# Mixing stage of a two-layer block on Trainium2: chunk states linked by a fading factor, and a turn that waits for less

## What is computed

```
q = layernorm(x);  k = v = ctx
log_D[s,t] = cums[s+1] - cums[t+1] + igate[t]   for t <= s, else -inf   (cums: running sum of log_sigmoid(fgate))
D  = exp(log_D - max_t log_D)
C  = (q k^T / 8) * D
h  = (C / (max(|sum_t C|, exp(-max log_D)) + 1e-6)) v
x += normalised h * outnorm_weight
```

## Time and profile before

| | us |
|---|---|
| median of 3 runs | 1862.72 (1861.0 to 1865.55) |
| the profiled execution, its own time | 1861.19 |
| span of that execution in the trace | 1859.5 |
| PE busy | 1683.3 (91%) |
| DVE busy | 1192.0 (64%) |
| ACT busy | 842.8 (45%) |
| POOL busy | 619.9 (33%) |

### The profile page before, as it was taken

One profiled execution on the slowest core, in us unless ns is written; L12 is line 12 of the kernel. 1 busy time (PEld: TensorE's weight loads), 2 busy tenths in 40 slices (PEclk: granted clock), 3 DMA queues, 4 the chain that ended last, 5 costly groups with the idle time before them and its releaser, 6 DMA issues. The chain is left out here.

```text
span 1859.5 us, 26060 instructions
## 1 busy us (share of the span) xinstructions
PE 1683.3 (91%) x8890; PEld 1152.6 (62%) x8890; DVE 1192.0 (64%) x2642; ACT 842.8 (45%) x1870; POOL 619.9 (33%) x746
## 2 busy tenths in 40 slices
PE   6469999996999999999999999999999999873584
PEld 4357777764666666666666666666666666572352
DVE  6444454432777777777777777777777777667761
ACT  3324443431555555555555555555555555421110
POOL 2154444430333232333333233232323232210375
PEclk9669999997999999999999999999999999955797
DMA  7100000003323222232323223232322223144144
GB/s 258 21 22 13 12 12 1 1 0 105 69 46 69 53 61 64 51 69 46 69 48 67 56 58 68 46 69 46 68 51 64 58 57 69 23 146 132 44 85 57
DMA packets 66657, 109.46 MB, mean 59 GB/s; under 512 B 16088, under 2 KB 48096, under 8 KB 66528
## 3 DMA queue, kind: packets, MB, share of 16 engines
q1 hardware_dynamic: 60384, 99.29, 21.8%
q0 software_dynamic: 6144, 8.52, 2.8%
HBM read 27.84 MB, written 12.85 MB: 22 GB/s over the span
## 5 line engine op out<-in xcount | busy, mean ns | idle before, releaser
L1030 POOL TENSOR_SCALAR at_Pr<-at_Pr,at_rinv 128x512 f32<-128x512 f32 x512 | 354.1, 692 | 826.7 <-DVE at_rinv L1057 826.7
L1009 ACT ACTIVATE at_Pr<-at_ps,at_nmax 128x512 f32<-128x512 f32 x512 | 352.0, 687 | 522.7 <-DVE at_nmax L1052 521.1
L1052 DVE TENSOR_REDUCE at_nmax<-at_ps 128x1 f32<-128x512 f32 x512 | 350.9, 685 | 139.0 <-PE at_ps L917 128.0
L917 PE MATMUL at_ps<-at_k,at_q 128*128 128x512 f32 x1024 | 420.8, 492 | 9.7 <-DMA at_k<-at_k_own 8.0
L928 PE MATMUL at_ps<-k_ident,at_Pr 128*128 128x128 f32 x2048 | 310.5, 274 | 4.0 <-POOL at_Pr L1030 4.0
L928 PEld LDWEIGHTS at_ps<-k_ident,at_Pr 128*128 128x128 f32 x2048 | 249.5, 140 | 93.2 <-POOL at_Pr L1030 32.8
L1064 DVE COPY at_PT<-at_ps 128x512 f32<-128x512 f32 x384 | 261.3, 681 | 0.0
L917 PEld LDWEIGHTS at_ps<-at_k,at_q 128*128 128x128 f32 x1024 | 174.6, 191 | 129.6 <-issue 120.1
L938 PE MATMUL at_ps<-at_PT,at_V 128*64 128x512 f32 x1024 | 233.8, 598 | 0.9 <-DVE at_PT L1064 0.9
L1057 DVE RECIPROCAL at_rinv<-at_rsum 128x1 f32<-128x1 f32 x512 | 83.3, 163 | 174.5 <-ACT at_Pr L1009 172.5
L938 PEld LDWEIGHTS at_ps<-at_PT,at_V 128*64 128x64 f32 x1024 | 67.7, 136 | 121.5 <-issue 120.3
(11 more groups left out here) (237 smaller groups left out, 2030.5 us busy)
## 6 DMA issues: line engine op xcount, KB each, us to landing
at_k<-at_k_own SPq DMA_DIRECT2D x256, 256.0 KB, 4.1
k_x<-in_x SPq DMA_DIRECT2D x8, 512.0 KB, 7.8
mg_ctx<-in_ctx SPq DMA_DIRECT2D x8, 512.0 KB, 8.0
mx_ctxn<-in_ctx SPq DMA_DIRECT2D x8, 512.0 KB, 3.9
rows<-lo_xn SPq DMA_DIRECT2D x8, 512.0 KB, 3.0
out<-k_x SPq DMA_DIRECT2D x1, 4096.0 KB, 14.6
r_w<-in_L_ffn_w SPq DMA_DIRECT2D x16, 256.0 KB, 5.6
mx_w<-in_L_ffn_w SPq DMA_DIRECT2D x2, 1024.0 KB, 9.8
```

The lines of the kernel that those rows point to most:

```text
L917: ins = pe.matmul(ps[:, S_BANK + j % 2, :], q2[:, u % 2, h, q:q + P], k2[:, u % 2, h, part, :], start=part == 0, stop=part == 1)
L1009: act.activation(Pr[:, j % 4, :], ps[:, S_BANK + j % 2, :], ACT.Exp, bias=nmax[:, j % 4:j % 4 + 1], accum_out=rsum[:, j % 4:j % 4 + 1]).th ...
L1030: pool.tensor_scalar(Pr[:, n % 4, :], Pr[:, n % 4, :], rinv[:, n % 4:n % 4 + 1], 1.0, ALU.mult, ALU.mult).then_inc(s["pn"], 1)
L1052: dve.tensor_reduce(nmax[:, j % 4:j % 4 + 1], ps[:, S_BANK + j % 2, :], AX.X, ALU.max, negate=True).then_inc(s["nmax"], 1)
```

## The change

It makes each state from the one before it. `states` computes only what each chunk adds (3 matmuls of one key tile each, weighted for the chunk's own end), and DVE adds to each the state before it times a fading factor, with two `scalar_tensor_tensor` instructions, each behind a wait for the one before. The factor is the decay's last column of each chunk, copied by `scale_queries` out of the bank that `spread_decay` filled. For that, `spread_decay` and `scores` move ahead of `states` on PE, `scale_queries` ahead of `keep_states` on DVE (and ahead of the input side's statistics), and `mapped(b, 3, 0)` ahead of the output side's turn. That turn waits for the first of the second unit's three `state` counts, the one instruction that reads U_BANK; `values` waits for all. The weights `aa`, the transposes and `weigh_keys` shrink to one tile per chunk.

```diff
-KIND_G, KIND_FLOOR, KIND_A = 0, TPB, (2 * TPB, 2 * TPB + 1, 2 * TPB + 3)
-KINDS = 2 * TPB + 6
+KIND_G, KIND_FLOOR, KIND_A = 0, TPB, 2 * TPB
+KINDS = 3 * TPB - 1
...
-                for k in range(6):
-                    at = R * (KIND_A[0] + k)
+                for k in range(TPB - 1):
+                    at = R * (KIND_A + k)
                     pe.transpose(ps[:, COL_BANK, at:at + R], aa[:, k, :], ident[0:R, 0:R])
...
-                    act.activation(aa[:, (0, 1, 3)[t]:(1, 3, 6)[t], :].rearrange("r a p -> r (a p)"),
-                                   gg[:, 0:P * (t + 1)], ACT.Exp, bias=neg_r[:, t:t + 1])
+                    act.activation(aa[:, t, :], gg[:, P * t:P * t + P], ACT.Exp, bias=neg_r[:, t:t + 1])
...
+    LINKS = TPB - 1
+        fade = sb("fade", [P, 2, TPB - 2], F32)
...
                 def states(m, p):
                     pe.wait_ge(s["kw"], m + 1)
                     pe.wait_ge(s["va"], m + 1)
-                    wait_count(pe, s["qs"], PAIRS * m + p)
-                    for k in range(TPB - 1):
-                        for t in range(k + 1):
-                            at = KIND_A[k] - KIND_A[0] + t
-                            ins = pe.matmul(ps[:, U_BANK, PV * k:PV * k + PV], kw[:, at, P * p:P * p + P],
-                                            vaug[:, t, 2 * p:2 * p + 2, :].rearrange("p h d -> p (h d)"),
-                                            start=t == 0, stop=t == k)
+                    pe.wait_ge(s["qs"], PAIRS * m + p + 1)
+                    for t in range(TPB - 1):
+                        ins = pe.matmul(ps[:, U_BANK, PV * t:PV * t + PV], kw[:, t, P * p:P * p + P],
+                                        vaug[:, t, 2 * p:2 * p + 2, :].rearrange("p h d -> p (h d)"),
+                                        start=True, stop=True)
                     ins.then_inc(s["u_ps"], 1)
...
                 def spread_decay(m, p):
-                    pe.wait_ge(s["state"], PAIRS * m + p + 1)
+                    wait_count(pe, s["state"], LINKS * (PAIRS * m + p))
...
                 def values(m, p):
-                    pe.wait_ge(s["qs"], u + 1)
+                    pe.wait_ge(s["state"], LINKS * (u + 1))
...
                     if mix:
                         spread_max(m, 0)
-                        states(m, 0)
+                        spread_decay(m, 0)
+                        scores(m, 0)
                     if mlp:
                         mapped(b, 0, 1)
                     if mix:
                         spread_max(m, 1)
+                        states(m, 0)
                     if mlp:
                         mapped(b, 1, 0)
-                    if mix:
-                        spread_decay(m, 0)
-                        scores(m, 0)
-                    if mlp:
                         mapped(b, 1, 1)
...
                         spread_max(m, 3)
-                        states(m, 1)
+                        spread_decay(m, 1)
+                        scores(m, 1)
                     if mlp:
                         mapped(b, 2, 1)
                     if mix:
-                        spread_decay(m, 1)
-                        scores(m, 1)
+                        states(m, 1)
                     done = min(m + 1, B)
+                    if mlp:
+                        mapped(b, 3, 0)
                     wait_count(pe, s["exp"], MH * done)
-                    wait_count(pe, s["qs"], PAIRS * done)
+                    wait_count(pe, s["state"], LINKS * PAIRS * done - LINKS + 1)
                     if there(b - 1):
                         wait_count(pe, s_in["out"], min(b + 1, B))
                         wait_count(pe, s_out["out"], b - 1)
                         turn(s_out, b - 1, tmp_out)
-                    if mlp:
-                        mapped(b, 3, 0)
                     if mix:
                         values(m, 1)
...
-                    for k in range(TPB - 1):
-                        at = KIND_A[k] - KIND_A[0]
...
-                        ins = pool.tensor_tensor(
-                            kw[:, at:at + k + 1, :].rearrange("p t (h d) -> p t h d", h=MH),
-                            ctxn[:, m % 2, 0:k + 1, :].rearrange("p t (h d) -> p t h d", h=MH), w, ALU.mult)
-                    ins.then_inc(s["kw"], 1)
...
+                    pool.tensor_tensor(
+                        kw[:, :, :].rearrange("p t (h d) -> p t h d", h=MH),
+                        ctxn[:, m % 2, 0:TPB - 1, :].rearrange("p t (h d) -> p t h d", h=MH), w, ALU.mult
+                    ).then_inc(s["kw"], 1)
...
                 def keep_states(m, p):
                         [P, TPB - 1, PV]), ALU.mult).then_inc(s["state"], 1)
+                    for t in range(1, TPB - 1):
+                        dve.wait_ge(s["state"], LINKS * u + t)
+                        dve.scalar_tensor_tensor(out=state[:, p, t, :], in0=state[:, p, t - 1, :],
+                                                 scalar=fade[:, p, t - 1:t], in1=state[:, p, t, :],
+                                                 op0=ALU.mult, op1=ALU.add).then_inc(s["state"], 1)
...
                 def scale_queries(m, p):
+                    dve.tensor_copy(fade[:, p, :], ps[:, U_BANK, 0:S - 2 * P].rearrange("p (t i) -> p t i", i=P)[:, :, P - 1])
...
                     if there(m):
-                        keep_states(m, 0)
+                        scale_queries(m, 0)
                     if there(b + 1):
                         dve.wait_ge(s["xadd"], b + 2)
                         norm_stats_dve(dve, s_in, b + 1, x_all, tmp_in)
                     if there(m):
-                        scale_queries(m, 0)
+                        keep_states(m, 0)
                         weigh(m, 0)
                         weigh(m, 1)
...
                     if there(m):
+                        scale_queries(m, 1)
                         keep_states(m, 1)
-                        scale_queries(m, 1)
                         weigh(m, 2)
                         weigh(m, 3)
```

More of the change, by code:

```diff
@@ L180, in mlstm_gates @@
             sb(n, [R, S], F32) for n in "ig fg absf efg lfg cums g gmax logmax floor bb".split())
-        aa = sb("aa", [R, 6, P], F32)
+        aa = sb("aa", [R, TPB - 1, P], F32)
         neg_r = sb("neg_r", [R, TPB], F32)
@@ L394, in mix_and_mlp @@
         vaug = sb("vaug", [P, TPB, MH, V1], F32)
-        kw = sb("kw", [P, 6, D], F32)
+        kw = sb("kw", [P, TPB - 1, D], F32)
+        fade = sb("fade", [P, 2, TPB - 2], F32)
         Dm = sb("Dm", [P, 2, S], F32)
@@ L642, in weigh_keys @@
                         wait_apart(pool, s["pv"], PAIRS * m)
-                    for k in range(TPB - 1):
-                        at = KIND_A[k] - KIND_A[0]
-                        w = g["cols"][:, KIND_A[k]:KIND_A[k] + k + 1, MH * m:MH * m + MH].rearrange(
-                            "p t (h a) -> p t h a", a=1).broadcast_to([P, k + 1, MH, MD])
-                        ins = pool.tensor_tensor(
-                            kw[:, at:at + k + 1, :].rearrange("p t (h d) -> p t h d", h=MH),
-                            ctxn[:, m % 2, 0:k + 1, :].rearrange("p t (h d) -> p t h d", h=MH), w, ALU.mult)
-                    ins.then_inc(s["kw"], 1)
+                    w = g["cols"][:, KIND_A:KIND_A + TPB - 1, MH * m:MH * m + MH].rearrange(
+                        "p t (h a) -> p t h a", a=1).broadcast_to([P, TPB - 1, MH, MD])
+                    pool.tensor_tensor(
+                        kw[:, :, :].rearrange("p t (h d) -> p t h d", h=MH),
+                        ctxn[:, m % 2, 0:TPB - 1, :].rearrange("p t (h d) -> p t h d", h=MH), w, ALU.mult
+                    ).then_inc(s["kw"], 1)
                 def add_heads(m):
```

## The result

**Slower, by 0.8%.** The changed kernel took 1876.9 us in the median of four runs (1876.0 to 1878.84), beside 1861.86 (1860.43 to 1865.55) for the kernel before on the same chip: a ratio of 1.0079, 95% interval 1.0062 to 1.0097. The forecast was 1872, range 1855 to 1880. The profiled execution is the longest of the four, 1878.84, with a span of 1877.1 us.

A forecast was written before the change was run, and what follows sets the result against it. PE, busy throughout steps 1 to 5 at full clock, bounds the kernel. Terms -0.4, -2.0, -0.2, -0.2, +3.9 and +1.3 give +2.4, with the clock's +8.0 +10.4, on 1861.19: 1872 us, range 1855 to 1880.

The forecast's parts named there:

- The hold of the first link: Second unit, steps 1 to 5: POOL's add_row holds the first DVE link to its end; values waits 1.97 us.
- The rival "not held": Links run beside POOL's add_row at 0.1 us a step in place of 1.97; total 1853.6 us; chance 0.22.
- The states: PE, each unit: six records of states in place of twelve, 0.67 us left of 1.34; 1.34 saved a step.
- The rival by which that saving is not made: PE is bound by something beside states, so six fewer records save nothing; about 1871 us; chance 0.05.
- The net of a step at full clock: Steps 1 to 5: 1.20 us gained, 1.97 lost waiting, +0.8 a step, +3.9 for five.
- The free chain: DVE's states, links and C with nothing in the way: C at T + 2.73, PE at T + 2.65; 0.1 us a step.
- The clock: Steps 1 to 5: after the wait PE's clock may fall; 1.6 us a step, +8.0 for five, between 0 and +15.
- The rival in which the clock stays up: Links held, but the clock does not fall in steps 1 to 5; 1863.6 us, no change; chance 0.15.
- The start: Before step 0: gate phase -0.4 us, step -2 -2.0, step -1 -0.2, with 2 either way for the clock.
- The clock here can fall elsewhere than today: 2 either way: Start of the kernel: the granted clock may fall at other places than before, worth 2 us either way.
- the +0.3 of step -1: Step -1: the second unit's links meet the input side's add_row on POOL, costing 0.3 us.
- Step 0 and step 6: Step 0: 1.0 of the 1.20 us gain lost, -0.2; step 6: output turn directly before input turn, +1.3.

The follow-up runs named there:

- e1: Changed kernel with POOL's addition of the output side's row moved ahead of the third mask; 1862.45 us, ratio 1.0.
- e4: Changed kernel with POOL's output-side addition replaced by a fill of a spare tile, which only writes SBUF (output bias left out); 1862.44 us, one run.
- e5: Changed kernel with POOL's output-side addition split into four instructions of 256 columns; 1865.32 us, ratio 1.001.
- e7: Changed kernel with POOL's addition ahead of the mask, C's products ahead of the states, and step 6's old place of the output turn; 1855.8 us, ratio 0.9954.
- e2: Kernel before with the new order of work on PE and DVE alone: twelve records in states, no links; 1862.86 us, ratio 0.9999.
- e3: Changed kernel with 18 transposes into unused PSUM ahead of the second unit's values, where PE waited; 1869.69 us, ratio 1.004.
- e6: Changed kernel with the second unit's two C products on DVE ahead of its states and links; 1860.38 us, ratio 0.9983.
- e10: Changed kernel with only e8's transposes added in steps -2 and -1; 1868.52 us, ratio 1.0023.
- e8: e7's kernel with transposes added where PE waits in steps -2 and -1, to keep the clock up; 1845.05 us, ratio 0.9903.
- e9: Kernel before with only e8's transposes added in steps -2 and -1; 1860.63 us, ratio 0.9987.

## Why the prediction was right, and where it was not

The mechanism of the forecast was right: a link that POOL holds, a wait of PE behind it, and a clock that falls after the wait. The profiled execution came out 17.6 longer where 10.4 was forecast. Of the 7.2 between them the start has 3.2, attention 2.7 and steps 1 to 5 1.1.

**The hold of the first link: right, in time and in length.** With T for the start of the `mapped(b, 3, 0)` behind `states`, the forecast had the link ready at T + 0.80, ended about T + 2.99 by POOL's `add_row`, and C at T + 4.62. With T = 202.54 they came at 203.34 (T + 0.80), 205.57 (T + 3.03) and 207.16 (T + 4.62); PE idled 2.00, forecast 1.97. That this agrees to 0.03 is partly luck: the sum left out 0.15 between C's end and `values`, and it had the output turn end at T + 2.65, where it ended at T + 2.77 (204.27 + 1.04). e1 (order), e4 (read or write) and e5 (length of one instruction) show that it is this addition, and by e4 its reading, that holds the link. The rival "not held" fell for that reason. Its condition was the right one: once POOL is done by T + 0.9, as in e1, the links are free.

**The states: right.** 0.67 a unit; e7 against e2 gives the 1.34 a step. The change of neighbours was put at 0.14 and cost 0.05 (e2). The rival by which that saving is not made is out.

**The net of a step at full clock: +0.95, forecast +0.8.** The saving was better, 1.29 gross (40.64 less e7's 39.35); the wait was dearer, 2.24 in place of 1.97: when PE then idles, the last transposes are paid to their end, 1.04, whereas in e7 `values` begins 0.87 after their start (203.59 to 204.46), and the first four records of `values` take 0.63 (the row at 207.31), not 0.56:

```profile
203.59 1.04 PE L437 MATMUL mm_ps<-k_ident,mm_xn 128*128 128x128 f32 x8
204.46 0.56 PE L508 MATMUL mm_ps<-mm_vaug,mm_C 128*128 128x65 f32 x4
```

Five steps give +4.7, forecast +3.9.

**The free chain was mis-sized.** The forecast let it cost 0.1 with nothing in the way; in e1 it costs 0.36 (39.71 against 39.35). A link took 0.355, not 0.30, and `values` begins 0.15 after C's end (207.71 to 207.86 in e1), the same hand-over that the sum left out. On top of it PE pays for the transposes that run to their end.

```profile
206.43 1.28 DVE L738 SCALAR_TENSOR_TENSOR mm_C<-mm_ps,mm_Dm 128x512 f32<-128x512 f32 x2
```
```profile
207.86 0.63 PE L508 MATMUL mm_ps<-mm_vaug,mm_C 128*128 128x65 f32 x4
```

**The clock: right in sum, wrong in form.** +8.0 was forecast as 1.6 in each of five steps. It came as 3.30, 3.29, 0, 0 and 1.65, together 8.2, after the same pause of 2.00 in each. That the sums agree to 0.2 is luck: 1.6 was a middle between a fall and none, and nothing in the forecast says how many steps fall. e3 shows that it takes PE standing still to lower the clock here, and e5 and e6 that pauses of 0.72 and 0.78 do not do so in these steps. Why steps 3 and 4 were spared stays open; their rows show the same pause, and in e10 the same two steps were spared. The rival in which the clock stays up is what e3 builds, at 208.0 for the five steps.

**The start: the step that failed.** The forecast had -0.4, -2.0 and -0.2, with 2 either way for the clock; it was +0.58, outside that by 1.2. The work did shrink, and by more than forecast: `values` of step -2 began at 76.05 for a forecast of 78.1. The gate phase, counted from the row to the end of the copy of its columns, took 8.53 in place of 9.06, 0.5 less for a forecast of 0.4. One part of the lead was not seen: the cast of `pick_half` on DVE, ahead of those `values`, took 3.19 in place of 4.50, beside a key weighting on POOL of 1.47 in place of 4.02:

```profile
65.83 4.50 DVE L818 CAST mm_pick_half<-k_ident 32x2048 fp32r<-32x2048 f32 x2
```
```profile
64.87 3.19 DVE L819 CAST mm_pick_half<-k_ident 32x2048 fp32r<-32x2048 f32 x2
```

But the clock, which comes up at about 78 before the change, came up only at about 85, and in between `values` lost 2.2; from there to the second unit's `values` it took 7.31 (80.75 to 88.06) in place of 5.30 (82.51 to 87.81), with 1.1 of the difference in the scores. Together that is the whole lead of 4.0. It is not one execution alone: e1, e3, e4 and e5 have the same steps -2 and -1, and in their profiles step 0 began at 130.10 to 131.77, the clock of the start between 0.52 and 0.58. e8 shows how much of the start hangs on the clock: with more work on PE it takes 10.9 less. So the term of the sum that failed is "The clock here can fall elsewhere than today: 2 either way". Why the clock came up later stays open.

The clock is not all, though. e6 and e7 begin step 0 at 128.18 and 128.37, 2.6 to 2.8 before the changed kernel, with the clock of the start at 0.58 and 0.57, hardly above its 0.56 (e5, at 0.58 too, begins it at 130.10): with C ahead of the links the second units wait 1.64 to 1.99 in place of 2.73. So states and links ahead of C in the second units, with no MLP for PE to work on meanwhile, had a price in the start too, and the sum has no term for it but the +0.3 of step -1. Of its terms for step -1, the 1.51 of the earlier trace rows did go, to 0.19, and the +0.3 did not come: the second unit's links ran at 0.35 each, after the input side's `add_row`.

**Step 0 and step 6: right.** Step 0 came to -0.07 for a forecast of -0.2, with the idle 1.00 before its second `values`, as expected. Step 6 came to +1.38 for +1.3, with a wait of 1.16 before its second turn; e2 shows it without the links, and e7 takes it away.

**Attention, +2.7, was in no step.** Nothing there differs between the kernels, and over the profiles its length lay between 1187.4 (before) and 1191.2 (e9, which has the old kernel's attention too), so no cause is put on it. The medians differ by 15.0 where the profiled executions differ by 17.6.

## What to carry to other kernels

Before a short operation is put on DVE with both inputs in SBUF, lay its time of readiness beside POOL's timeline: a POOL addition that streams its operands from SBUF held it here to the addition's own end, and the price is that wait and all that is queued behind it. The better cure here was the order, not the size: with the POOL work ahead of the meeting 0.12 of the wait was left (e1), and with what does not need the held result ahead of it on DVE as well, none (e7); with POOL's addition in quarters 0.72 was left (e5). In a stage where PE waits often, such as the start here, the mean granted clock lay between 0.52 (e1) and 0.90 (e8) with the waits, so a saving there is read only with the clock beside it.

## What the runs showed of the hardware

- A fill of 2048 columns on POOL (1.81) had two links of 0.35 run inside it (e4); an addition of 1024 columns held one for 2.23.
- A mask on POOL held a link too: in every kernel with links, the first link of the first unit of steps 0 to 5 took 0.78 beside a mask of 0.63 to 0.64 that began with it; it lies under `mapped`, and PE has no wait there.
- The same pause of 2.00 before `values` in five steps lowered the clock in three of them (after, and the same three in e10); the pause filled with 18 transposes lowered it in none (e3).
